# First unit of a seven-product matmul kernel: position 3 ahead of position 2, W11 loaded in four pieces, sums of W1 on VectorE, idle transposes at the start, logits' transposes later

## The chip, the cores and the metric

The kernel runs on one core of one Trainium2 chip. A core has TensorE (PE in the profile; its weight loads are PEld), VectorE (DVE), ScalarE (ACT), GpSimd (POOL), SyncE (SP, which here only issues DMAs) and 16 DMA engines. The metric is the device time of the one core in microseconds (us). Lower is better. All numbers come from measured executions or from one profiled execution of the program.

## The reference

The input u has shape (4, 1024, 1024); everything is float32. What matters of the reference:

```
xn = layernorm(u)                                   # over the last axis
g  = sigmoid(xn @ gate_w.T + gate_b);  u_g = xn * g
y  = c * G * cumsum(b * u_g / G) + (d + mean(u_g) @ lr_u @ lr_v / 4) * u_g
h  = silu(xn @ w1.T);  h = silu(h @ w3.T);  h = h @ w2.T
routes = top-2 of softmax(xn @ wr.T) over 8 experts; gates = the two, normalised
out_ffn[:] = 0;  out_ffn[expert] += gate * h        # summed over all 4096 tokens, so only rows 0..7 differ from 0
return u + y * silu(out_ffn)                        # rows 8.. are just u
```

Only eight rows of the result differ from the input, but the routed sum runs over all 4096 tokens, so the products with w1 and w3 are computed in full. The product with w2 is made once, after the sum. The gate is needed for the first 1024 tokens alone.

## The kernel before, in words

**Units.** Work is cut in nine units n of 1024x1024x1024: units 0 to 3 multiply the four batches by w1, unit 4 is the gate, units 5 to 8 multiply h by w3. The plan works with 2x2 blocks of 512 and takes seven block products instead of eight. The seven are the positions i = 0..6; each needs a sum or difference of x blocks (steps "T") and one of weight blocks (steps "S"). Positions are grouped in chains that share an accumulator bank: `CHAINS = ((0, 1), (2,), (3, 4), (5, 6))`. A position has four tiles j, each 128 output rows by 512 columns, contracted over four slices k of 128.

**Precision.** Each operand is split into a rounded part and a rest. "WH" and "HI" are ScalarE's rounded copies (weights, x), "WO" and "LO" are VectorE's subtractions for the rest. A tile is three matmuls per k (lines 944 to 946), so 12 matmuls of 512 columns. PSUM has five banks for tiles (`main`), two for logits (`lgp`) and one `spare`. VectorE or ScalarE empties a finished tile (step "PO") into `s1`, `u3` or the output tile `o`; the step "ST" then stores tiles that are final.

**Unit 0** is special: x comes as rows, is normalised on the chip and transposed. There are eight row blocks t of 128 tokens. "ROW" loads one (512 KB), "NA" computes its mean and variance on VectorE (bn_stats) and GpSimd (the power -0.5), "NS" does the same with ScalarE sums and GpSimd, "NB" normalises on VectorE, "TR" transposes on TensorE (two groups of four), "TE" copies the result out of PSUM on ScalarE (two copies per group for t < 4, one for t >= 4), "TL" makes the rest on VectorE. Position 0 of unit 0 is done in two halves of 256 columns, steps "MP" (half, j). Position 2 needs f = a - b + d of the x blocks: steps "TQ" (two VectorE operations per t), then "HQ" (rounded copy) and "LZ" (rest). "XS" stores x blocks for unit 4.

**Order.** `plan()` writes one list of steps by hand. Every engine walks that list and does its own part of each step, strictly in the order of the list, with semaphore waits. So a late step holds up everything behind it on its engine. The first part (lines 236 to 245) is written out; from then on the tiles follow in order and `at(n, i, j, step)` puts extra steps behind the tile (n, i, j).

**Other steps around the change.** "WL" loads a 512x512 block of weights (1 MB), in the order 11, 12, 22, 21 for w1. "SP" (lines 769 to 778) makes two sums of w1 blocks on GpSimd. "LQ" computes logits with TensorE, "LE" copies them to SBUF on ScalarE, "RA" transposes them back on TensorE, "RT" reduces them on VectorE. "STAT" are ScalarE's sums over rows of units 1 to 3, "MVC", "MV" and "BC" turn them into mean and rstd, "LN" (VectorE, two operations over 128x2048) normalises a block. `places_of` hands out nine buffers for x blocks.

Of the kernel before, what the change touches and what calls it, by code (L numbers as in the profile page):

```python
# [12 lines left out]
E = 8  # L13
# [30 lines left out]

CHAINS = ((0, 1), (2,), (3, 4), (5, 6))
CHAIN_OF = (0, 0, 1, 2, 2, 3, 3)
# [20 lines left out]
def lo_place(n, i):  # L67
    return "l2" if n == 0 and i == 2 else LO_PLACE[i]
# [6 lines left out]
def plan():  # L75
# [7 lines left out]
    for n in range(NN):  # L83
        ln = 0 < n < GATE
        if n == 0:
            at(0, 1, 0, "TR", 6)
            at(0, 1, 0, "TE", 6, 0)
            at(0, 1, 0, "TE", 6, 1)
            at(0, 1, 0, "TQ", 2)
# [3 lines left out]
            at(0, 1, 1, "TQ", 3)  # L93
            for t in range(4):
                at(0, 1, 2, "HQ", t)
                at(0, 1, 2, "LZ", t)
# [28 lines left out]
            at(0, 3, 2, "RT", 0)
            at(0, 5, 0, "RT", 1)
        else:
# [97 lines left out]
    for k in range(3):  # L225
# [10 lines left out]
    steps = [("ROW", 0), ("ROW", 1), ("ROW", 2), ("WL", 0, 2, "11"), ("ROW", 3), ("ROW", 4), ("ROW", 5), ("WL", 0, 6, "12"),  # L236
# [9 lines left out]
    gate_tiles = [(i, j) for i in OUT_OF for j in range(4)]  # L246
    tiles = [(n, i, j) for n in range(NN) for i in range(7) for j in range(4)]

    def behind(k):

        if k < 0:
            return
        n, i, j = tiles[k]
        if n or i:
            steps.append(("PO", n, i, j))

# [13 lines left out]
    for k, (n, i, j) in enumerate(tiles):  # L270
# [3 lines left out]
        out_of(k - 2)  # L274
        if j == 1:
# [3 lines left out]
        steps.extend(extra.pop((n, i, j), []))  # L279
# [11 lines left out]
def places_of(steps):  # L291
# [11 lines left out]
    for s in steps:  # L303
# [8 lines left out]
        elif s[0] == "HI":  # L312
# [3 lines left out]
        elif s == ("TQ", 0):  # L316
            take(0, "f")
        elif s == ("HQ", 0):
            take(0, "h2", "l2")
        if s == ("T", 0, 4):  # L320
            free.append((place[(0, "f")], s))
        elif s[0] in ("ST", "GX") and s[2:] == (4, 3):
            free.append((place[(s[1], "o")], ("o", s[1])))
        elif s == ("MP", 1, 3) or s[0] == "MM" and s[3] == 3:
            n, i = s[1:3] if s[0] == "MM" else (0, 0)
            for name in (f"h{i}", lo_place(n, i)):
                free.append((place[(n, name)], 7 * n + i))
# [9 lines left out]
def program(nc, x, xT, wB, w2T, small, out):  # L337
# [43 lines left out]
    with ExitStack() as ctx:  # L381
# [115 lines left out]
        s_pa = sem("s_pa")  # L497
        s_pv = sem("s_pv")
# [69 lines left out]
        def vacated(wait, n, name):  # L568
# [21 lines left out]
        def x_in(wait, n, i):  # L590
# [3 lines left out]
            elif n == 0 and i == 2:  # L594
# [4 lines left out]
        def s_in(wait, w, k):  # L599

            if w == 0 and k in (1, 3):
                wait(s_sp, nth("SP", 0, k))
            else:
                wait(s_s, nth("S", w, k))
# [36 lines left out]
        def bank_free(wait, n, i, j):  # L641
# [3 lines left out]
            if was[1] < 2:  # L645
                wait(s_pa, pa(*was))
            else:
# [16 lines left out]
        def _(eng):  # L664
            wait = Waiter(eng)
            ncopy = 0
            for s in steps:
                kind = s[0]
                if kind == "ROW":
# [5 lines left out]
                    eng.dma_start(row_buf(r), x[r * P:(r + 1) * P, :]).then_inc(s_row[r if r < 8 else 4 + r % 2], 16)  # L675
                elif kind == "CST":
# [64 lines left out]
        def _(eng):  # L741
# [20 lines left out]
            for s in steps:  # L762
# [44 lines left out]
        def _(eng):  # L807
# [14 lines left out]
            for s in steps:  # L822
                kind = s[0]
                if kind == "TE":
# [7 lines left out]
                    eng.activation(xf(0, b)[:, :, ts], bk, ACT.Copy).then_inc(s_ter, 1)  # L832
                elif kind == "HQ":
                    t = s[1]
                    vacated(wait, 0, "h2")
                    wait(s_tq, nth("TQ", t))
                    ts = slice(t * P, (t + 1) * P)
                    eng.activation(xr(0, "h2")[:, :, ts], xf(0, "f")[:, :, ts], ACT.Copy).then_inc(s_hq, 1)
# [8 lines left out]
                elif kind == "WH":  # L847
                    w, p = s[1:]
                    src = w_from(w, p)
                    if p in (0, 1, 4):  # L850
                        wait(s_wl[{0: 2, 1: 6}.get(p, p) if w == 0 else p], wloads[(w, {0: 2, 1: 6}.get(p, p) if w == 0 else p)])
                    else:
                        s_in(wait, w, {5: 1, 2: 2, 3: 3, 6: 4}[p])
                    if w == 0 and p >= 4:
                        wait(s_tr, 2 * (8, 4, 2)[p - 4])
                    eng.activation(w_r(p, 0), src, ACT.Copy).then_inc(s_wh, 1)
                elif kind == "PO":
                    n, i, j = s[1:]
# [80 lines left out]
        def _(eng):  # L939
            wait = Waiter(eng)  # L940
            wait(s_id, 2)
# [6 lines left out]
            for s in steps:  # L948
                kind = s[0]
                if kind == "TR":  # L950
# [4 lines left out]
                    for h in range(2):  # L955
                        for q in range(4):
                            k = 4 * h + q
                            mm = eng.transpose(tr_banks(t)[h][:, q * P:(q + 1) * P], row_buf(t)[:, k * P:(k + 1) * P],
                                               ident[:, :])
                        mm.then_inc(s_tr, 1)  # L960
                elif kind == "MP":
                    half, j = s[1:]
                    wait(s_wo, nth("WO", 0, 0))
                    wait(s_tel, nth("TL", 2 * half + 1, 0))
                    ts = slice(2 * P * half, 2 * P * (half + 1))
                    xh, xl = xr(0, "h0"), xr(0, "l0")
                    wh, wl = w_r(0, 0), w_r(0, 1)
                    js = slice(j * P, (j + 1) * P)
                    for k in range(4):
                        mm = three(main[bank[(0, 0, j)]][:, ts], wh[:, k, js], wl[:, k, js], xh[:, k, ts], xl[:, k, ts],  # L970
                                   half == 0 and k == 0, False)
                    if half:
                        mm.then_inc(s_mm, 1)
# [422 lines left out]
```

## Time and profile before

| | us |
|---|---|
| median of 3 runs | 793.51 (792.91 to 794.73) |
| the profiled execution, its own time | 793.97 |
| span of its trace, first to last instruction | 792.2 |
| TensorE busy | 756.0 |
| VectorE busy | 514.2 |
| ScalarE busy | 353.0 |
| GpSimd busy | 54.0 |
| DMA, mean over the span | 148 GB/s |

Times in the rows are us from the start of the span. The busy time of TensorE is no measure of its speed: it is also busy at half clock. What counts is when a position starts, and how long TensorE takes from there to the next.

### The profile page before, as it was taken

The page shows a single profiled execution, that of the slowest core. Times are in us where ns is not written, and L with a number is a line of the kernel's source. Part 1 is how long each engine was busy: PE and PEld are TensorE (multiplying, and loading weights), DVE is VectorE, ACT ScalarE, POOL GpSimd, SP SyncE. Part 2 cuts the span into 40 slices and gives each one's busy share as a digit, 9 for nine tenths or more (in the row PEclk, how much of TensorE's full clock was granted, in tenths as well). Part 3 has the DMA queues.
Part 4 walks back from the last instruction along what each step waited for, and adds up shares of the span by engine and source line. Part 5 has one row for each costly group of instructions (what it writes and reads, how often), then busy time and mean ns, then how long its engine had stood idle before and what let it go on. Part 6 is the DMA issues. An engine that isn't in the chain of part 4 may idle for free.

```text
span 792.2 us, 8750 instructions
## 1 busy us (share of the span) xinstructions
PE 756.0 (95%) x3510; PEld 595.8 (75%) x3510; DVE 514.2 (65%) x557; ACT 353.0 (45%) x459; POOL 54.0 (7%) x57
## 2 busy tenths in 40 slices
PE   2889999799999999999998999999999999999996
PEld 2767886588778877888887877877787778777873
DVE  5689877666676758728799999475624553455322
ACT  6678846724675434423582346223323241334121
POOL 2530022102030200000000000000000000000000
PEclk9999999899999999999999999999999999999999
DMA  9634556245624353555775652304230414110500
GB/s 359 232 146 149 200 201 211 84 152 184 218 85 156 117 195 113 187 208 165 289 284 180 231 208 107 134 0 186 85 139 16 186 39 154 47 54 0 214 1 2
DMA packets 26968, 117.20 MB, mean 148 GB/s; under 512 B 3392, under 2 KB 3632, under 8 KB 19760
## 3 DMA queue, kind: packets, MB, share of 16 engines
q1 hardware_dynamic: 17712, 99.87, 34.5%
q10 hardware_dynamic: 9216, 16.78, 5.7%
q8 instruction: 27, 0.44, 0.2%
q14 instruction: 13, 0.11, 0.0%
HBM read 95.60 MB, written 37.77 MB: 168 GB/s over the span
## 4 chain that ended last, share of the span: by engine, by line
PE 77%; DVE 13%; issue 3%; ACT 3%; DMA 2%; POOL 1%; SPq 0%; ACTq 0%; DVEq 0%; POOLq 0%
PE main L944 24%; PE main L945 23%; PE main L946 23%; PE lgp L1005 1%; DVE x5f L1091 1%; DMA wl6f<-wB 1%; PE spare L1032 1%; PE lgp L1032 1%; DVE x4f L1091 1%; DMA wh5f<-x 1%; DVE x8f L1091 1%; DVE s L1091 1%; DVE x0r L1091 1%; DVE x3r L1091 1%; DVE rows L1134 1%
## 5 line engine op out<-in xcount | busy, mean ns | idle before, releaser
L1091 DVE TENSOR_TENSOR s<-s,main 128x512 f32<-128x512 f32 x72 | 48.9, 683 | 67.0 <-PE main L946 66.8
L1091 DVE TENSOR_TENSOR u<-u,main 128x512 f32<-128x512 f32 x36 | 24.5, 686 | 50.7 <-PE main L946 50.7
L879 ACT ACTIVATE s<-s 128x512 f32<-128x512 f32 x32 | 20.1, 630 | 58.2 <-DVE s L1091 58.2
L879 ACT ACTIVATE u<-u 128x512 f32<-128x512 f32 x32 | 20.1, 632 | 58.2 <-DVE u L1091 58.2
L1091 DVE TENSOR_TENSOR u<-s,main 128x512 f32<-128x512 f32 x36 | 24.4, 684 | 30.6 <-PE main L946 30.5
L879 ACT ACTIVATE rows<-rows 128x512 f32<-128x512 f32 x16 | 10.1, 632 | 67.9 <-DVE rows L1091 67.8
L864 ACT ACTIVATE s<-main 128x512 f32<-128x512 f32 x36 | 20.7, 593 | 41.9 <-PE main L946 21.7
L1091 DVE TENSOR_TENSOR rows<-s,main 128x512 f32<-128x512 f32 x16 | 11.0, 688 | 31.2 <-PE main L946 31.2
L820 ACT ACTIVATE rows<-rows,nm 128x1024 f32<-128x1024 f32 x24 | 27.7, 1153 | 0.8
L818 ACT ACTIVATE rows<-rows 128x1024 f32<-128x1024 f32 x26 | 27.3, 1050 | 0.1
L879 ACT ACTIVATE u<-main 128x512 f32<-128x512 f32 x32 | 18.7, 590 | 18.3 <-PE main L946 18.3
L945 PE MATMUL main<-x3r,wh0r 128*128 128x256 f32 (+1 forms) x64 | 22.5, 352 | 0.0
L944 PE MATMUL main<-x2r,wh0r 128*128 128x256 f32 (+1 forms) x48 | 17.0, 353 | 4.4 <-DVE x3r L1091 4.4
L804 POOL MEMSET tail<- 128x1024 f32 x1 | 1.0, 954 | 269.1 <-PE main L946 269.1
L792 POOL TENSOR_SCALAR mvu<-acs 128x4 f32<-128x4 f32 x6 | 5.9, 981 | 193.6 <-ACT rows L820 193.6
L946 PE MATMUL main<-x2r,wl0r 128*128 128x256 f32 (+1 forms) x48 | 16.2, 338 | 0.0
L944 PEld LDWEIGHTS main<-x2r,wh0r 128*128 128x128 f32 x48 | 10.2, 212 | 5.4 <-DVE wl0r L1091 4.8
L945 PEld LDWEIGHTS main<-x3r,wh0r 128*128 128x128 f32 x64 | 13.2, 207 | 1.2
L944 PE MATMUL main<-x2r,wh2r 128*128 128x512 f32 x32 | 12.9, 402 | 0.6 <-DVE x3r L1091 0.6
L945 PE MATMUL main<-x4r,wh4r 128*128 128x512 f32 x32 | 13.2, 412 | 0.0
L944 PE MATMUL main<-x4r,wh3r 128*128 128x512 f32 x32 | 12.6, 392 | 0.0
L946 PE MATMUL main<-x2r,wl2r 128*128 128x512 f32 x32 | 12.5, 390 | 0.0
(691 smaller groups left out, 2443.7 us busy)
## 6 DMA issues: line engine op xcount, KB each, us to landing
out<-x SPq DMA_DIRECT2D x31, 512.0 KB, 7.8
rows<-x SPq DMA_DIRECT2D x26, 512.0 KB, 4.2
H_d<-u ACTq DMA_DIRECT2D x32, 256.0 KB, 3.7
H_d<-s ACTq DMA_DIRECT2D x16, 256.0 KB, 2.9
rows<-xh_d SPq DMA_DIRECT2D x16, 256.0 KB, 4.9
w2f<-w2T SPq DMA_DIRECT2D x2, 2048.0 KB, 11.2
wl2f<-wB SPq DMA_DIRECT2D x3, 1024.0 KB, 8.3
wl6f<-wB SPq DMA_DIRECT2D x3, 1024.0 KB, 8.3
```

Source lines behind the costliest of these rows:

```text
L792: eng.tensor_scalar(mvu[:, h, 0, :], acs[:, h, 0, :], 1.0 / D, None, ALU.mult)
L818: link(eng.activation(row, row, ACT.Copy, accum_out=total))
L820: return eng.activation(where, row, ACT.Square, bias=nm[:, 0:1], accum_out=square)
L864: eng.activation(s1[:, j, :], bk, ACT.Copy).then_inc(s_pa, 1)
L879: ins = eng.activation(dst, src, ACT.Silu)
L944: eng.matmul(o, sh, mh, start=first, stop=False, skip_group_check=True)
L945: eng.matmul(o, sh, ml, start=False, stop=False, skip_group_check=True)
L946: return eng.matmul(o, sl_, mh, start=False, stop=last, skip_group_check=True)
L1005: mm = eng.matmul(lgp[h][Q * q:Q * (q + 1), :], wr32[:, NQ * kh + q, :], xf(n, b)[:, q, :], start=(kh == 0), stop=(kh == 1))
L1032: mm = eng.matmul(acc[o][Q * j:Q * (j + 1), :], Pz[:, 8 * u + 4 * h + j, :], c_buf(n, i, j), start=(u == 0 and h == 0), stop=(u == NU - 1 ...
L1091: return eng.tensor_tensor(o, a, b, op)
L1134: eng.tensor_scalar(row_buf(t), row_buf(t), mv0[:, t, 0:1], mv0[:, t, 1:2], ALU.subtract, ALU.mult).then_inc(s_nb, 1)
```

## The change

- The chains of unit 0 become (0, 1), (3,), (2,), (4,), (5, 6): position 3 (x part d - b) comes before position 2. Position 3's tiles are copied to `u3` by ScalarE, position 2's are added to `s1` by VectorE, position 4 adds `u3`, and a new step "PU" adds `s1` to `u3`. The per-t path TD, HQ, LZ now serves position 3 with one subtraction per t; f = a + (d - b) is one whole operation later (T, 0, 2).
- W11 comes as four 256 KB DMAs (W0) ahead of rows 2 and 3, with its own split steps WH0 and WO0, and MP goes by (half, k) with all four j inside, so that a piece k is enough to start.
- Block 21 of w1 goes to another buffer; the sums 1 and 3 of w1 move from GpSimd ("SP", removed) to VectorE ("S").
- 34 transposes of the identity into `spare` open TensorE's list ("WARM").
- NA and NS are dealt out anew, and the extra steps of unit 0 are moved.
- Around unit 1: HI and LO of its first blocks, LN a, LQ a and c, RA of its second logits and the STAT rows stand at other tiles.

```diff
-CHAINS = ((0, 1), (2,), (3, 4), (5, 6))   # still used for n > 0
+CHAINS0 = ((0, 1), (3,), (2,), (4,), (5, 6))
...
         if n == 0:
             at(0, 1, 0, "TR", 6)
+            at(0, 1, 0, "LZ", 0)
             at(0, 1, 0, "TE", 6, 0)
             at(0, 1, 0, "TE", 6, 1)
-            at(0, 1, 0, "TQ", 2)
+            at(0, 1, 0, "LZ", 1)
+            at(0, 1, 0, "NB", 7)
+            at(0, 1, 0, "TD", 2)
+            at(0, 1, 0, "HQ", 2)
+            at(0, 1, 0, "WO", 0, 3)
...
+            at(0, 1, 3, "T", 0, 2)
+            at(0, 1, 3, "S", 0, 1)
...
+            at(0, 2, 0, "S", 0, 2)
+            at(0, 2, 0, "HI", 0, 2)
+            at(0, 2, 0, "WH", 0, 2)
+            at(0, 2, 0, "LO", 0, 2)
+            at(0, 2, 1, "WO", 0, 2)
             for b in "acbd":
-                at(0, 2, 0, "LQ", 0, b)
+                at(0, 2, 1, "LQ", 0, b)
+            at(0, 2, 2, "T", 0, 4)
             at(0, 2, 2, "HI", 0, 4)
+            at(0, 2, 3, "T", 0, 1)
+            at(0, 2, 3, "LE", 0)
+            at(0, 3, 0, "S", 0, 4)
...
-            at(n, *((-1, 0) if first else (-2, 2)), "LO", n, 0)
-            at(n, *((-1, 3) if first else (-1, 0)), "HI", n, 1)
+            at(n, *((-1, 1) if first else (-2, 2)), "LO", n, 0)
+            at(n, *((-1, 2) if first else (-1, 0)), "HI", n, 1)
...
-                at(n, *((-2, 1) if first else (-4, 3)), "LN", n, "a")
+                at(n, *((-2, 3) if first else (-4, 3)), "LN", n, "a")
...
-                at(n, *((0, 0) if first else (-1, 1)), "LQ", n, "a")
-                at(n, *((0, 0) if first else (-1, 1)), "LQ", n, "c")
+                at(n, *((0, 1) if first else (-1, 1)), "LQ", n, "a")
+                at(n, *((0, 1) if first else (-1, 1)), "LQ", n, "c")
...
-                at(n, 2, 0, "RA", c + 1)
+                at(n, *((3, 0) if first else (2, 0)), "RA", c + 1)
...
-                when = [(0, i, j) for i, j in ((2, 0), (2, 0), (2, 2), (3, 0), (3, 2), (4, 0), (4, 2), (5, 0))]
+                when = [(0, i, j) for i, j in ((2, 1), (2, 3), (3, 0), (3, 1), (3, 3), (4, 0), (4, 2), (4, 3))]
...
-    steps = [("ROW", 0), ("ROW", 1), ("ROW", 2), ("WL", 0, 2, "11"), ("ROW", 3), ("ROW", 4), ("ROW", 5), ("WL", 0, 6, "12"),
-             ("ROW", 6), ("ROW", 7), ("WL", 0, 4, "22"), ("WL", 0, 3, "21"), ("CST", 0),
-             ("NA", 0), ("NS", 1), ("NA", 2), ("NB", 0), ("TR", 0), ("TE", 0, 0), ("TE", 0, 1), ("NB", 1), ("TR", 1), ("WH", 0, 0),
...
+    steps = [("WARM", 0), ("ROW", 0), ("ROW", 1)] + [("W0", k) for k in range(4)] + [("ROW", 2), ("ROW", 3), ("WL", 0, 6, "12"),
+             ("ROW", 4), ("ROW", 5), ("ROW", 6), ("ROW", 7), ("WL", 0, 5, "21"), ("WL", 0, 4, "22"), ("CST", 0),
+             ("NA", 0), ("NA", 1), ("NB", 0), ("TR", 0), ("NB", 1), ("TR", 1),
+             ("WH0", 0), ("WH0", 1), ("WH0", 2), ("WH0", 3), ("TE", 0, 0), ("WO0", 0), ("TL", 0, 0), ("NA", 2), ("TE", 1, 0), ("TL", 1, 0),
+             ("TE", 0, 1), ("TE", 1, 1), ("WO0", 1), ("WO0", 2), ("NA", 3), ("NB", 2), ("WO0", 3),
+             ("MP", 0, 0), ("MP", 0, 1), ("TR", 2), ("MP", 0, 2), ("MP", 0, 3), ("NA", 5), ("NB", 3), ("TR", 3),
+             ("NS", 4), ("TE", 2, 0), ("TE", 2, 1), ("NA", 6), ("TL", 2, 0), ("TE", 3, 0), ("TL", 3, 0), ("TE", 3, 1),
+             ("MP", 1, 0), ("MP", 1, 1), ("NB", 4), ("TR", 4), ("MP", 1, 2), ("MP", 1, 3), ("WH", 0, 1),
+             ("XS", "a"), ("XS", "c"), ("TL", 0, 1), ("TL", 1, 1), ("TL", 2, 1), ("TL", 3, 1), ("NB", 5), ("TR", 5), ("WO", 0, 1),
+             ("TE", 4, 0), ("TE", 4, 1), ("NS", 7), ("PO", 0, 0, 0), ("PO", 0, 0, 1), ("PO", 0, 0, 2), ("PO", 0, 0, 3),
+             ("TE", 5, 0), ("TE", 5, 1), ("NB", 6), ("TD", 0), ("HQ", 0), ("S", 0, 3), ("WH", 0, 3), ("TD", 1), ("HQ", 1), ("ROW", 8), ("ROW", 9)]
...
+                elif kind == "W0":
+                    k = s[1]
+                    eng.dma_start(w_f(2, 1)[:, k, :], wB[0, 0, 0, :, k, :]).then_inc(s_w0[k], 16)
...
-                elif kind == "SP":
-                    k = s[2]
-                    for p in (3, 4) if k == 1 else (2,):
-                        wait(s_wl[p], wloads[(0, p)])
-                    if k == 1:
-                        ins = eng.tensor_tensor(w_f(5, 1), w_f(3, 1), w_f(4, 1), ALU.add)
-                    else:
-                        wait(s_sp, 1)
-                        ins = eng.tensor_tensor(w_f(3, 1), w_f(2, 1), w_f(3, 1), ALU.subtract)
-                    ins.then_inc(s_sp, 1)
...
+                if kind == "WARM":
+                    wait(s_id, 1)
+                    for q in range(34):
+                        eng.transpose(spare[:, q % 4 * P:(q % 4 + 1) * P], ident[:, :], ident[:, :])
+                    wait(s_id, 2)
...
+                elif kind == "PU":
+                    j = s[1]
+                    wait(s_p3, j + 1)
+                    wait(s_pv, pv(0, 2, j))
+                    tt(u3[:, j, :], u3[:, j, :], s1[:, j, :], ALU.add).then_inc(s_pv, 1)
```

In unit 0 the second argument of `at` is now the rank in the chain order, so `at(0, 2, ...)` stands at position 3 and `at(0, 3, ...)` at position 2.

## Rows read from the trace of the kernel before

**Rows 1.** Page, part 1: busy us, share of the span, instructions.
```profile
PE 756.0 (95%) x3510; PEld 595.8 (75%) x3510; DVE 514.2 (65%) x557; ACT 353.0 (45%) x459; POOL 54.0 (7%) x57
```

**Rows 2.** Waits of TensorE, whole run: us in total, times, longest us.
```profile
PE main L958 <- DVE wh6f L1134: 10.3, 1, 10.3
PE main L944 <- DVE x3r L1091: 5.0, 2, 4.4
PE lgp L1012 <- ACT lg L912: 4.6, 1, 4.6
PE lgp L958 <- DVE rows L1134: 3.9, 1, 3.9
PE main L944 <- DVE wl1r L1091: 2.3, 1, 2.3
```

**Rows 3.** Windows: length, busy (x) per engine, clock, DMA share, GB/s.
```profile
31.54:43.27 11.73, 5.52 (x32) 5.34 (x33) 11.73 (x5) 7.90 (x17) 10.89 (x4) 0.85 0.36 124
...
57.44:117.77 60.33, 60.33 (x285) 46.83 (x286) 49.69 (x38) 45.29 (x68) 5.78 (x6) 1.00 0.52 187
117.77:144.87 27.10, 26.70 (x133) 18.84 (x132) 21.77 (x12) 16.48 (x29) 6.64 (x3) 1.00 0.50 175
144.87:164.49 19.62, 15.05 (x54) 11.44 (x55) 10.65 (x8) 12.06 (x17) 0.00 (x0) 0.83 0.34 120
...
164.49:175.37 10.88, 10.88 (x49) 9.01 (x48) 6.98 (x7) 4.40 (x6) 0.00 (x0) 1.00 0.42 146
```

**Rows 4.** Timeline of VectorE: start, us, instruction, idle before.
```profile
30.38 5.01 DVE L1134 TENSOR_SCALAR rows<-rows,mv 128x1024 f32<-128x1024 f32 x1 [2.11 <-POOL mv L785]
...
43.09 2.28 DVE L1091 TENSOR_TENSOR wh6f<-wl5f,wl2f 128x2048 f32<-128x2048 f32 x1
...
66.10 0.68 DVE L1091 TENSOR_TENSOR s<-s,main 128x512 f32<-128x512 f32 x1
```

**Rows 5.** Timeline of GpSimd.
```profile
30.31 4.53 POOL L774 TENSOR_TENSOR wl5f<-wl3f,wl4f 128x2048 f32<-128x2048 f32 x1
```

**Rows 6.** Timeline of all engines, first 10 us.
```profile
3.95 0.69 DVE L1128 BATCH_NORM_STATS2 bst<-wh6f 128x6 f32<-128x512 f32 x1 [3.95 <-DMA wh6f<-x]
...
5.25 1.06 ACT L818 ACTIVATE wh6f<-wh6f 128x1024 f32<-128x1024 f32 x1 [3.23 <-DMA wh6f<-x]
...
5.89 0.58 POOL L768 TENSOR_TENSOR mv<-mv,mhalf 128x1 f32<-128x1 f32 x1
...
7.96 0.69 DVE L1128 BATCH_NORM_STATS2 bst<-wh5f 128x6 f32<-128x512 f32 x1 [2.48 <-DMA wh5f<-x]
...
9.41 1.48 DVE L1134 TENSOR_SCALAR wh6f<-wh6f,mv 128x1024 f32<-128x1024 f32 x2
```

**Rows 7.** DMA issues on SyncE: start, us to issue.
```profile
2.13 0.44 SPq L683 DMA_DIRECT2D wl2f<-wB  x1
...
4.32 1.19 SPq L683 DMA_DIRECT2D wl6f<-wB  x1
```

**Rows 8.** DMA issues, first 12 us: KB each, median us to landing.
```profile
wl2f<-wB SPq DMA_DIRECT2D x1, 1024.0 KB, 8.3
...
wl6f<-wB SPq DMA_DIRECT2D x1, 1024.0 KB, 12.4
```

**Rows 9.** Timeline of ScalarE.
```profile
24.53 0.60 ACT L830 ACTIVATE x2r<-lgp 128x512 fp32r<-128x512 f32 x1 [0.31 <-PE lgp L958]
...
26.45 1.08 ACT L818 ACTIVATE rows<-rows 128x1024 f32<-128x1024 f32 x1
...
29.04 1.90 ACT L856 ACTIVATE wh1r<-wl6f 128x2048 fp32r<-128x2048 f32 x1
...
48.51 1.28 ACT L879 ACT_TABLE_LOAD   x1
```

**Rows 10.** Chain of waits, start and us: two matmuls of 256 columns.
```profile
19.35 0.21 PE main L944
...
22.87 0.12 PE main L946
```

More of the change, by code:

```diff
@@ L67, in lo_place, with chains, order, rank @@
 def lo_place(n, i):
-    return "l2" if n == 0 and i == 2 else LO_PLACE[i]
+    return f"l{i}" if n == 0 and i in (2, 3) else LO_PLACE[i]
+def chains(n):
+    return CHAINS if n else CHAINS0
+def order(n):
+    return [i for c in chains(n) for i in c]
+def rank(n, i):
+    return 7 * n + order(n).index(i)
 def layer_of(n):
@@ L255, in behind @@
             steps.append(("PO", n, i, j))
+        if n == 0 and i == 2 and j == 3:
+            for t in range(4):
+                steps.append(("PU", t))
     def out_of(k):
@@ L274, in plan @@
         out_of(k - 2)
+        p = rank(n, i) % 7
         if j == 1:
@@ L315, in places_of @@
             take(s[1], "f")
-        elif s == ("TQ", 0):
+        elif s == ("TD", 0):
             take(0, "f")
         elif s == ("HQ", 0):
+            take(0, "h3", "l3")
+        elif s == ("HI", 0, 2):
             take(0, "h2", "l2")
-        if s == ("T", 0, 4):
-            free.append((place[(0, "f")], s))
+        if s in (("T", 0, 4), ("T", 0, 1)):
+            free.append((place[(0, "f" if s[2] == 4 else "b")], s))
         elif s[0] in ("ST", "GX") and s[2:] == (4, 3):
@@ L488, in program @@
         s_t = sem("s_t")
+        s_w0 = [sem(f"s_w0{k}") for k in range(4)]
+        s_wh0 = sem("s_wh0")
+        s_wo0 = sem("s_wo0")
         s_wh = sem("s_wh")
@@ L573, in vacated @@
                 wait(s_t, nth(*was))
+                wait(s_hi, nth("HI", 0, 2))
+                wait(s_lo, nth("LO", 0, 2))
+            elif was == ("T", 0, 1):
+                wait(s_t, nth(*was))
+                wait(s_lq, nth("LQ", 0, "b"))
+                wait(s_xs[2], 16)
             elif isinstance(was, tuple):
@@ L599, in s_in, with w_in, mm @@
         def s_in(wait, w, k):
-            if w == 0 and k in (1, 3):
-                wait(s_sp, nth("SP", 0, k))
-            else:
-                wait(s_s, nth("S", w, k))
+            wait(s_s, nth("S", w, k))
+        def w_in(wait, w, i):
+            if w == 0 and i == 0:
+                wait(s_wo0, 4)
+            else:
+                wait(s_wo, nth("WO", w, i))
+        def mm(n, i, j):
+            return 4 * rank(n, i) + j + 1
         def pv(n, i, j):
@@ L646, in bank_free @@
                 wait(s_pa, pa(*was))
+            elif was[:2] == (0, 3):
+                wait(s_p3, was[2] + 1)
             else:
@@ L967, in _ @@
                     wh, wl = w_r(0, 0), w_r(0, 1)
[L968 to L973, printed above, removed]
+                    for j in range(4):
+                        js = slice(j * P, (j + 1) * P)
+                        ins = three(main[bank[(0, 0, j)]][:, ts], wh[:, k, js], wl[:, k, js], xh[:, k, ts], xl[:, k, ts],
+                                    half == 0 and k == 0, False)
+                        if half and k == 3:
+                            ins.then_inc(s_mm, 1)
                 elif kind == "MM":
@@ L978, in _ @@
                     bank_free(wait, n, i, j)
-                    if n == 0 and i == 2:
+                    if n == 0 and i == 3:
                         wait(s_ter, 16)
-                    wait(s_wo, nth("WO", w, i))
+                    w_in(wait, w, i)
                     x_in(wait, n, i)
@@ L985, in _ @@
                     js = slice(j * P, (j + 1) * P)
-                    begins = i in (0, 2, 3, 5)
+                    begins, ends = (i in [c[e] for c in chains(n)] for e in (0, -1))
                     for k in range(4):
-                        first, last = begins and k == 0, not begins and k == 3 or i == 2 and k == 3
+                        first, last = begins and k == 0, ends and k == 3
                         if n < L2:
-                            mm = three(o, wh[:, k, js], wl[:, k, js], xh[:, k, :], xl[:, k, :], first, last)
+                            ins = three(o, wh[:, k, js], wl[:, k, js], xh[:, k, :], xl[:, k, :], first, last)
                         else:
-                            mm = three(o, xh[:, k, js], xl[:, k, js], wh[:, k, :], wl[:, k, :], first, last)
-                    mm.then_inc(s_mm, 1)
+                            ins = three(o, xh[:, k, js], xl[:, k, js], wh[:, k, :], wl[:, k, :], first, last)
+                    ins.then_inc(s_mm, 1)
                 elif kind == "LQ":
@@ L1169, in _ @@
                         raw_in(wait, n, X_FROM[i])
+                    elif (n, i) == (0, 2):
+                        vacated(wait, 0, "l2")
+                        wait(s_t, nth("T", 0, 2))
                     elif i != 6:
@@ L1189, in _ @@
                             wait(s_xs[0], 16)
+                            wait(s_t, nth("T", 0, 2))
                         if n < GATE:
@@ L1192, in _ @@
                         ins = tt(a, b, a, ALU.subtract)
+                    elif (n, k) == (0, 2):
+                        raw_in(wait, 0, "a")
+                        wait(s_hq, 4)
+                        wait(s_lz, 4)
+                        ins = tt(xf(0, "f"), xf(0, "f"), a, ALU.add)
                     elif k == 2:
@@ L1283, in _ @@
                         dst = c_buf(n, 4, j)
+                        if n == 0:
+                            wait(s_pv, pv(0, 3, j))
+                            old = u3[:, j, :]
                     elif i == 5:
```

175 lines of the change are left out of this document (91 added, 84 removed), and 7 rows, old and new, of the table steps.

## The prediction

> **What bounds the kernel now.** I read the busy shares first, then TensorE's waits, then the windows between the starts of positions, and last the queues of VectorE, ScalarE and GpSimd where a wait ends. TensorE is busy 95% of the span [rows 1], so only two things can move the time: TensorE waiting, and TensorE at half clock. Of the waits, five lie before unit 1 has passed its third position [rows 2]: 10.3 us for the first normalised rows, 4.4 of the 5.0 us for the first rest of x and of W11, 3.9 for the normalised row block 3, 2.3 for the rest of W12, and 4.6 in unit 1 for the copy of the logits. In steady state a position takes 10.88 us, the window 164.49:175.37 [rows 3]; position 2 of unit 1 took 19.62, at a mean clock of 0.83 [rows 3]. The 3.9 us wait has its cause on GpSimd: VectorE's normalisation, which takes 0.74 us elsewhere (1.48 for two) [rows 6], took 5.01 while GpSimd ran its sum of 128x2048, 4.53 us [rows 4, 5]. In 31.54:43.27 GpSimd and VectorE are busy side by side for 10.9 us and TensorE only for 5.5 [rows 3]. All the rest behind 164.49 is untouched by the diff.
>
> **The walk through the new start.** I go through the new list engine by engine. Units of cost: a ScalarE copy of 128x512 0.48 (four between 24.53 and 26.45), NS 2.59 (26.45 to 29.04), a weight copy 1.9 [rows 9]; a VectorE operation over 128x2048 2.2, over 128x512 0.61 (2.28 and 0.68 less 0.07 overlap with the next) [rows 4]; NA 1.5 (two of 0.69 and the aggregate, estimated 0.2), NB 0.74, GpSimd's part 0.9 [rows 6]. A matmul of 256 columns is 0.12 at full and 0.21 at half clock [rows 10], so MP of one k (12 matmuls) is 1.43 or 2.56, and a TR of eight transposes about 0.9 or 1.75 (estimated, a transpose being as long as a 256-column matmul).
>
> *Loads.* R1 is there at 5.25, R2 at 7.96 [rows 6]; W11, with 2.62 MB issued up to it, at 2.13 + 8.3 = 10.4, W12, with 5.24 MB, at 4.32 + 12.4 = 16.7 [rows 7, 8]. By the same bytes the last piece of W11 now lands at about 9.2 (2.1 MB), R2 10.4, R3 11.7, R4 15.3, R5 16.7, R6 17.8, R7 18.9. Bounds for the pieces: 7.6 (in strict order) to 10.4. The four issues take 0.44 each [rows 7], faster than the data flow.
>
> *Rows 0 and 1.* NA 0 from 3.95, NA 1 from 5.5 to 7.0, NB 0 to 7.8: today NB 0 stands behind NA 2, which waits for R2, and starts at 9.41 [rows 6]. TR 0 at 7.8 instead of 10.3, TR 1 9.3 to 10.2 (GpSimd's part beside NB 0 taken at up to 1.5). ScalarE rounds the pieces by 9.75, then TE 00 to 10.8, TE 10 to 11.8. VectorE: TL 00, NA 2 (R2), TL 10 to 13.6. So MP starts at **13.7**; before, the waits of 10.3 and 4.4 us stood ahead of it [rows 2].
>
> *Clock.* The 34 idle transposes start at about 1.6 and last 3.7 to 7.2 us, so they end by 8.8 at the latest; they cost at most 1 us on TR 0, hidden by the pieces. But TensorE then idles from 10.2 to 13.7, about 3.5 us. In this trace the clock fell to 1.2 GHz with the waits of 3.9 and 4.6 us: the mean clocks of the windows that hold them are 0.85 and 0.83, against 1.00 in the windows without such a wait [rows 2, 3]. I take the half clock for the first 3.6 us: +1.35 us on the walk below. The Trainium skill ("TensorE: Matmul & The Clock Gate", What's actually happening) says that the chip's look at activity runs free of the kernel, so that the same kernel warms at another matmul from run to run; by that the 1.35 could be 0 or double, and this trace can't decide it, being one execution.
>
> *Position 0.* At full clock: MP 00, 01 to 16.6; TR 2 (NB 2 at 17.0) to 18.0; MP 02, 03 to 20.9; TR 3 to 21.8; NS 4 holds ScalarE 15.3 to 17.9, TE 2 to 20.0, TE 30 at 22.4, TL 30 at 23.1; MP 10 at 23.25, then TensorE has work: MP 11 26.1, TR 4 27.0, MP 12, 13 29.85, TR 5 30.75. ScalarE's NS 7 and PO(0,0,0) end at 30.7, so position 1 starts at **30.8** (43.27 before: the end of that window). W12's copy and rest are ready at 29.2.
>
> *Position 1* takes 10.9 and two TR (1.8). TR 7 waits for NB 7 behind LZ 1, behind HQ 1 (ScalarE, 36.0): 0.3 us of stall. TE 7 comes behind PO(0,1,0) with the table load of 1.28 [rows 9], and HQ 3, LZ 3 end at 43.0. Position 3 starts at **43.8**, with the half clock at **45.2**; today the third position starts at 57.44. The sum that this took from GpSimd, S 3, is at 30.6 to 32.8 on VectorE beside MP and PO: hidden; slack of its user WO(0,3) 4 us. **Gain of the front: 57.44 - 45.2 = 12.2** (bounds: 6, if the pieces land with today's W11, 1.2 us later, and ScalarE's queue slips by 5, two NS; and 13.6 with the clock held).
>
> *The five positions to unit 1* have the same content as in 57.44:117.77, 60.33 us without a wait [rows 3]. VectorE gets S 1, S 2, LO 2, WO 2, T 2 and four PU there (5 x 2.2 + 4 x 0.61 = 13.4 us) and loses WO 3, T 3, LO 3 (6.6). Walking VectorE's and ScalarE's lists I find the last operand of position 2 ready 4 us ahead, of position 4 3 us, of position 5 5 us, of position 6 6 us. The tightest is LO(1,0): LN a starts 13.2 us before unit 1, then LN c, PO, LO(1,0) end 0.7 us before it. Cost 0 (up to 1.5 if it slips). Cover gone, each us late is a us of stall.
>
> *Unit 1.* RA of its second logits goes from the first tile of position 2 to that of position 3, some 11 us later, and the copy that it waited for was 4.6 late: the wait goes. With it goes the half clock behind it. Position 2 should take 10.88 + 0.7 (RA, MV) = 11.6 instead of 19.62: 8.0; the 0.4 idle in 117.77:144.87 (27.10 against 26.70 busy) goes too, since VectorE reaches LO 2 about 23 us after the start of the unit, position 2 being due at 25.8. **Gain 8.4** (bounds 0 and 8.4). Moving the STAT rows costs nothing: ScalarE is busy 45 of 60 us there, and their last is due 8 us before the mean is used.
>
> *Sum:* 12.2 + 8.4 = 20.6. Own time of the profiled execution 793.97 - 20.6 = 773.4; the median of the runs is 0.46 below that execution, so **773.0**.
>
> **Rivals.**
> - *The boundary wait only moves.* LO(1,0) or HI(1,1) slips past its 0.7 us, since LN a now comes two tiles later and VectorE has more to do; TensorE then waits some 4 us and comes back at half clock as it did behind RA. For: the thin slack. Against: each of VectorE's durations is measured and it idled here before. Gain 12.2 + 0.4: 793.5 - 12.6 = **781**.
> - *ScalarE sets the pace of the front.* NS 4, TE 2 and 3, NS 7 and PO(0,0,0) stand in one queue with no slack at 30.7. A row that lands 2 us later and 2 to 4 us of such slips leave a front gain of about 7: 793.5 - 15.4 = **778**.
> - *Slower than before: TensorE stays at 1.2 GHz until position 3.* The front now has many short waits (before MP, TR 2, TR 3, MP 10, TR 7) where the old one had a few long ones. At half clock 96 matmuls cost 0.09 more, 8.6, 48 of 512 columns 0.2 more, 9.6, eight TR 0.85 more, 6.8: 25.0, of which 1.35 is counted: 773.0 + 23.6 = **797**. It turns slower from about 20 of these 25 us on. For: the mean clock of 0.85 today. Against: from MP 10 on there is work without a gap, and every window without a long wait has a mean clock of 1.00 [rows 3].
> - *The front's gain is given back at unit 1*: LN a there waits for the sums of its rows (STAT 8 to 11, GpSimd, MV, BC) and their loads, which come no earlier. Against: by the walk they have 4 us or more to spare. Unit 1's gain alone stays: 793.5 - 8.4 = **785**.
>
> **How the numbers follow.** Forecast 0.55 (its own range 770 to 776), ScalarE 0.20, boundary 0.17, loads of the sums 0.05, half clock 0.03. The range 768 to 782 holds the first three but for their tails; its low end adds the held clock (1.35) and the doubts of the walk on the good side. Runs of this kernel can tell 0.2% (1.6 us) from no change: faster 0.95, same 0.02, slower 0.03.
>
> **What would show it.** MP's first matmul near 13.7; its spacing there 0.21 or 0.12; position 1 at 31 to 32, position 3 at 44 to 46, unit 1 at 104 to 107; no GpSimd row over 128x2048; no NB above 1 us; no wait of L1012 in unit 1 and position 2 there in about 11.6 us. Wrong would be a new wait of more than 1 us between position 3 of unit 0 and position 3 of unit 1, or a first MP behind 16.

## The result, and the profile after

The changed kernel takes 775.0 us, the median of 4 runs (774.69 to 776.75), beside 793.21 us (792.54 to 794.73) for the kernel before on the same chip: ratio 0.9772, 95% interval 0.9752 to 0.9793. It is 18.2 us faster, where 20.5 were forecast (773.0), and the time lies in the range of 768 to 782. The profiled execution took 776.75 us with a span of 774.8 (792.2 before).

The page of the kernel after, part 1, answers to [rows 1]: TensorE's busy time is the same 756 us, its share is 98% instead of 95.

```profile
PE 756.1 (98%) x3544; PEld 596.9 (77%) x3544; DVE 510.9 (66%) x567; ACT 347.4 (45%) x451; POOL 40.3 (5%) x52
```

TensorE's waits, whole run of the kernel after (us in total, times, longest), answer to [rows 2]:

```profile
PE main L995 <- DVE x3r L1147: 6.6, 2, 5.1
PE main L995 <- DVE u L1147: 2.0, 1, 2.0
PE spare L1004 <- POOL ident L798: 1.6, 1, 1.6
...
PE main L1014 <- DVE wh6f L1190: 0.8, 1, 0.8
PE lgp L1014 <- DVE wh6f L1190: 0.4, 1, 0.4
```

The waits of 10.3, 3.9, 2.3 and 4.6 us are gone. One of 5.1 us stands ahead of the first MP, and one of 1.5 (6.6 less 5.1) ahead of MP (1, 0); the walk of the prediction has this second one too, from 21.8 to 23.25. The windows of the kernel after, cut where positions start (columns as in [rows 3]):

```profile
15.43:20.72 5.29, 5.29 (x25) 5.29 (x26) 5.22 (x11) 2.75 (x6) 2.42 (x4) 0.50 1.04 422
20.72:35.21 14.49, 13.00 (x106) 12.53 (x105) 11.32 (x17) 10.04 (x18) 3.51 (x8) 0.97 0.73 289
35.21:48.34 13.13, 13.08 (x64) 10.58 (x65) 9.39 (x11) 11.24 (x18) 2.58 (x3) 1.00 0.25 92
48.34:108.66 60.32, 60.32 (x286) 46.77 (x286) 53.77 (x40) 47.98 (x74) 3.73 (x6) 1.00 0.61 209
108.66:135.12 26.46, 26.46 (x133) 19.09 (x132) 23.74 (x12) 16.52 (x28) 6.51 (x3) 1.00 0.53 185
135.12:146.54 11.42, 11.42 (x51) 9.03 (x50) 7.05 (x7) 11.29 (x16) 0.00 (x0) 1.00 0.37 127
146.54:157.89 11.35, 11.35 (x54) 9.40 (x52) 8.42 (x7) 4.76 (x8) 0.00 (x0) 1.00 0.60 221
```

Read down the lengths: this is where the time came from. The starts before are those of the trace before.

| stretch | before | forecast | after | gained |
|---|---|---|---|---|
| to the first MP | 18.36 | 13.7 | 15.43 | 2.93 |
| first MP to position 1 | 24.91 | 18.45 | 19.78 | 5.13 |
| position 1 to the third position | 14.17 | 13.05 | 13.13 | 1.04 |
| five positions to unit 1 | 60.33 | 60.33 | 60.32 | 0.01 |
| unit 1 to its position 4 | 57.60 | 49.2 | 49.23 | 8.37 |
| the rest of the span | 616.83 | same | 616.91 | -0.08 |

The sum is 17.40, the difference of the spans (792.2 - 774.8).

How far can one trace be trusted with such starts? Two of the kernels below (a_ra_back, a_sums_on_gpsimd) leave TensorE's work up to position 1 as it is in the changed kernel, and start position 1 at 34.36 and 33.80 instead of 35.21. Two others (b_unit1_all, b_ra_only) do the same with the kernel before and start it at 43.90 and 42.59 instead of 43.27. So a difference of up to 1.4 us in the start of position 1 between two single traces shows nothing by itself.

### The profile page after: what moved, and what is told of

Its sections match the earlier page's. It is cut to its first block, busy times and chain, and to the rows that moved or that the text cites. A ratio compares the mean times of both kernels' runs of the same rounds, so it can differ in the third digit from the quotient of the medians.

```text
span 774.8 us, 8825 instructions
## 1 busy us (share of the span) xinstructions
PE 756.1 (98%) x3544; PEld 596.9 (77%) x3544; DVE 510.9 (66%) x567; ACT 347.4 (45%) x451; POOL 40.3 (5%) x52
## 4 chain that ended last, share of the span: by engine, by line
PE 85%; DVE 8%; issue 3%; DMA 2%; ACT 2%; SPq 0%; DVEq 0%
PE main L995 27%; PE main L997 26%; PE main L996 26%; PE lgp L1061 2%; DMA wl6f<-wB 1%; PE spare L1088 1%; DMA wl2f<-wB 1%; PE lgp L1088 1%; DVE x3r L1147 1%; DVE s L1147 1%; DVE x3f L1147 1%; DVE x0r L1147 1%; DVE x1r L1147 1%; DVE u L1379 1%; PE main L1122 0%
## 5 line engine op out<-in xcount | busy, mean ns | idle before, releaser
L1147 DVE TENSOR_TENSOR u<-s,main 128x512 f32<-128x512 f32 x32 | 21.7, 682 | 29.6 <-PE main L997 29.6
L912 ACT ACTIVATE s<-main 128x512 f32<-128x512 f32 x36 | 20.5, 594 | 44.5 <-PE main L997 19.0
L931 ACT ACTIVATE u<-main 128x512 f32<-128x512 f32 x32 | 18.6, 590 | 17.6 <-PE main L997 17.4
L995 PE MATMUL main<-x6r,wh3r 128*128 128x512 f32 x32 | 12.5, 392 | 0.0
L996 PE MATMUL main<-x6r,wh0r 128*128 128x512 f32 x32 | 12.5, 390 | 0.0
L996 PE MATMUL main<-x5r,wh1r 128*128 128x512 f32 x32 | 12.5, 390 | 0.0
L997 PE MATMUL main<-x6r,wl3r 128*128 128x512 f32 x32 | 12.5, 389 | 0.0
L996 PE MATMUL main<-x5r,wh2r 128*128 128x512 f32 x32 | 12.5, 389 | 0.0
```

The source lines that it names most:

```text
L931: ins = eng.activation(dst, src, ACT.Silu)
L995: eng.matmul(o, sh, mh, start=first, stop=False, skip_group_check=True)
L996: eng.matmul(o, sh, ml, start=False, stop=False, skip_group_check=True)
L997: return eng.matmul(o, sl_, mh, start=False, stop=last, skip_group_check=True)
L1147: return eng.tensor_tensor(o, a, b, op)
```

## The experiments

Each run is beside the kernel before on its chip; its time is the median of 4 or 5 runs. Code cuts are marked with "...".

**Unit 1's moves alone, on the kernel before.**

```diff
-                at(n, 2, 0, "RA", c + 1)
+                at(n, *((3, 0) if first else (2, 0)), "RA", c + 1)
...  # and the changed places of HI, LO, LN a, LQ a and c, STAT rows; nothing else of the change
```

> The kernel before with only the moves around unit 1 (HI, LO, LN a, LQ a and c, RA, STAT rows). My theory: this group is worth 8.4 us by itself, whatever the front does, so the ratio to before is 0.9895 (about 784.9 us), unit 1 up to its position 3 takes about 38 us instead of 46.7, and no wait of the logits' transpose is left. Rival: without the earlier start of the front the moves only shift VectorE's work and the wait comes back at LO of unit 1; then 788 to 793.

Measured: 785.83 (before 793.55), ratio 0.9903 (0.9886 to 0.9919). Unit 1 runs from 118.64 to its position 4 at 167.87, 49.23 us, the very figure of the changed kernel. The stage is 8.4 us shorter by the trace (57.60 before) and the median 7.7 lower; the 785.8 is 0.9 above what I expected, and position 1 starts 0.6 later in this trace, which is scatter. The group doesn't need the new front.

**RA alone, on the kernel before.** Only the changed line above.

> The kernel before with RA of unit 1's second logits alone moved from the first tile of position 2 to that of position 3. Theory: the wait of 4.6 us and the half clock behind it go with this one step, so 785.5 (8.0 less). Rival: the ScalarE copy it waited for is a sign of a late VectorE; then LO 2 or LO 3 of unit 1 makes TensorE wait instead, and only some 3 us are won (790).

Measured: 786.73, ratio 0.9915 (0.9899 to 0.9932). Position 2 of unit 1 takes 11.54 us instead of 19.62, by this kernel's window:

```profile
130.07:144.17 14.10, 13.70 (x69) 9.48 (x68) 13.86 (x8) 6.92 (x12) 6.28 (x3) 1.00 0.27 95
144.17:155.71 11.54, 11.54 (x50) 9.11 (x51) 6.84 (x5) 9.38 (x12) 0.00 (x0) 1.00 0.32 113
```

So one step moved by 11 us brings 7.6 of the 8.4 us (unit 1 to position 4: 49.99), and 6.8 by the medians, 1.2 less than I expected. The 0.4 us of idle in front of position 2 stays (14.10 against 13.70): that is what the other moves of the group remove, with another 0.35 in the stretches around.

**RA back, in the changed kernel.** The same line the other way.

> The changed kernel with RA of unit 1's second logits back at the first tile of position 2. In the changed kernel that tile ends at 137.9 and the copy that RA needs ends at about 140.1. Theory: a wait of 2.3 us comes back, without or with half clock behind it: 777.3 to 780. Rival: the earlier HI, LO and LQ steps alone removed the wait: 775.

Measured: 780.24 (777.79 to 781.59), ratio 0.9818 (0.9791 to 0.9845), a little above the 777.3 to 780 of the expectation. The wait returned, and with it, in this trace, the half clock:

```profile
PE lgp L1068 <- ACT lg L964: 2.4, 1, 2.4
```

Its window of position 2:

```profile
134.28:151.71 17.43, 14.98 (x55) 11.37 (x54) 8.59 (x7) 11.91 (x17) 0.00 (x0) 0.80 0.40 137
```

17.43 instead of 11.42: 2.4 of wait, 0.5 for the transposes themselves, which stand in position 3 otherwise (10.88 here, 11.35 there), and 3.1 of half clock. The four runs differ: two near 781.6 with a mean granted clock of 0.988 over the run, two at 777.8 and 778.9 with 0.992. The trace has the first kind: from unit 1 to its position 4 it takes 54.78 instead of 49.23, so a wait of 2.4 us cost 5.5. That in the other two the wait stood without the half clock is read from their mean clocks and times only; no trace shows it.

**The sums on VectorE, in the kernel before.**

```diff
-                        ins = eng.tensor_tensor(w_f(5, 1), w_f(3, 1), w_f(4, 1), ALU.add)       # GpSimd
+                        ins = tt(w_f(5, 1), w_f(3, 1), w_f(4, 1), ALU.add)                      # VectorE, same place; the other sum too
```

> The kernel before with its two GpSimd sums of W1 done by VectorE at the same two places. Theory: both engines were slowed by each other for 10.9 us; VectorE now needs 4.4 us more of its own and loses about 9 of stretched time, NB 3 takes 0.8 instead of 5.0, position 1 starts about 5 us earlier and no half clock follows: 787 to 789. Rival: VectorE was the bound of the front anyway, so its 4.4 us come in the place of the 3.9 us wait: 792 to 794.

Measured: 788.87, ratio 0.9944 (0.9927 to 0.996). Its VectorE, at the place of [rows 4]:

```profile
30.01 0.81 DVE L1124 TENSOR_SCALAR rows<-rows,mv 128x1024 f32<-128x1024 f32 x1 [2.12 <-POOL mv L775]
30.74 2.28 DVE L1081 TENSOR_TENSOR wl5f<-wl3f,wl4f 128x2048 f32<-128x2048 f32 x1
33.13 2.29 DVE L1081 TENSOR_TENSOR wl3f<-wl2f,wl3f 128x2048 f32<-128x2048 f32 x1
```

The normalisation takes 0.81 instead of 5.01 and each sum 2.3 where GpSimd took 4.5 to 4.8. Position 1 starts at 38.93 instead of 43.27 (42.59 and 43.90 in the two other traces with the front of before), and the third position at 53.32 instead of 57.44: some 4 us of the front come from this edit alone, 4.7 by the medians. Not as expected, half clock did follow: a wait of 4.0 us for the rest of W12 now stands ahead of position 1, where 2.3 stood, and position 1 has a mean clock of 0.88.

**The sums on GpSimd, in the changed kernel.**

```diff
-                elif kind == "S":                                       # VectorE
+                elif kind == "S" and s[1:] not in ((0, 1), (0, 3)):
...
+                elif kind == "S" and s[1:] == (0, 3):                   # GpSimd; (0, 1) alike
...
+                    eng.tensor_tensor(w_f(3, 1), w_f(2, 1), w_f(5, 1), ALU.subtract).then_inc(s_sp, 1)
```

> The changed kernel with sums 1 and 3 of W1 put back on GpSimd, at the places that the changed kernel gives them. Theory: sum 3 (near 35 us) now stretches VectorE's rest of W12, NB 6, NB 7 and the TD and LZ steps by some 4 us and position 1 or 3 starts 2 to 4 us later: 777 to 779. Rival: at those places VectorE has slack, so within 1 us of the changed kernel (775 to 776).

Measured: 782.0, ratio 0.986 (0.9843 to 0.9876), 7 us slower than the changed kernel, where I expected 2 to 4. GpSimd, then VectorE of this kernel, then TensorE's wait:

```profile
34.46 4.61 POOL L838 TENSOR_TENSOR wl3f<-wl2f,wl5f 128x2048 f32<-128x2048 f32 x1
39.15 4.85 POOL L842 TENSOR_TENSOR wl5f<-wl5f,wl4f 128x2048 f32<-128x2048 f32 x1
```

```profile
36.22 3.40 DVE L1163 TENSOR_TENSOR x8f<-x7f,x6f 128x512 f32<-128x512 f32 x1 [2.88 <-ACT x7f L889]
39.54 5.61 DVE L1163 TENSOR_TENSOR x3r<-x8f,x2r 128x512 fp32r<-128x512 f32 x2
```

```profile
PE lgp L1030 <- DVE wh4f L1206: 5.5, 1, 5.5
```

Three VectorE operations of 0.7 us each last 9 us. Position 1 takes 20.38 us instead of 13.13, with a mean clock of 0.83. I had counted one sum in reach; both ran there, one behind the other: GpSimd had no other step between them. That this is why the edit costs more in the new order than it gave in the old is argued, not tried.

**Without the idle transposes.**

```diff
-                    for q in range(34):
+                    for q in range(0):
```

> The changed kernel without the 34 transposes of the identity. In the changed kernel the first MP started at 15.43, at half clock, after an idle stretch of about 5 us. Theory: the transposes only make TR 0 and TR 1 faster (about 0.5 instead of 0.9 us per four), and MP waits for the copies behind the pieces of W11; so 0 to 0.7 us slower (775 to 775.7), and the first two MP take as long as now (5.3 us). Rival: they pay for the whole front, 2 us or more slower.

Measured: 775.12 (774.62 to 776.17), ratio 0.9767 (0.9749 to 0.9786): no difference. TR 0 and TR 1 end later (3.65 us of transposes from 8.14 instead of 2.05 from 7.71), and the first MP starts at 15.27 all the same. MP 00 and 01 take 4.85 us here and 5.29 in the changed kernel, beside 4.81 and 4.80 in a_ra_back and a_sums_on_gpsimd, which have the transposes. The transposes of the change buy nothing, as expected.

**Kept busy up to MP.**

```diff
+                    if t == 1:
+                        for q in range(46):
+                            eng.transpose(main[q % 4][:, 0:P], ident[:, :], ident[:, :])
```

> The changed kernel with 46 more transposes of the identity behind TR 1, into banks that MP then begins anew. Theory: the half clock of the first two MP (24 matmuls at 0.22 instead of 0.12) comes from the idle stretch ahead of them; kept busy, MP 00 and 01 take 2.9 instead of 5.3 us. What follows waits for rows 4 (ScalarE's NS 4, on its DMA), so of the 2.4 us between 0.5 and 2.4 come through: 772.6 to 774.5. Rival: the clock falls anyway or MP is late behind the added transposes: 775 to 776.

Measured: 775.27 (774.85 to 775.61), ratio 0.9764 (0.9747 to 0.9781): no difference, where I expected 0.5 to 2.4 us. The rival's time came, but not for its reason, since the clock held and MP was not late. The window of the first two MP in this kernel:

```profile
15.36:18.40 3.04, 3.04 (x28) 2.97 (x27) 3.01 (x7) 1.40 (x4) 1.30 (x2) 1.00 1.02 404
```

3.0 instead of 5.3 us, so the half clock there was the idle stretch's doing. From the first MP to position 1 it is 17.05 us instead of 19.78, 2.7 less, since TR 2 behind MP 01 ran at half clock as well. Position 1 starts at 32.41 instead of 35.21 and unit 2 at 190.40 instead of 193.19, yet the span is only 1.2 us shorter and the median not at all. Where the other 1.6 went: position 4 of the gate unit took 13.38 instead of 14.89 (1.5 better), and against that stood a new wait of 1.05 us on the gate's VectorE work, 0.7 in unit 5 and 1.25 in the tail. The tails, 9.07 after and 10.32 here, with the same work:

```profile
765.73:774.80 9.07, 3.60 (x32) 1.53 (x32) 1.54 (x3) 1.18 (x3) 0.00 (x0) 0.88 0.02 4
```

```profile
763.28:773.60 10.32, 4.87 (x32) 1.64 (x32) 1.54 (x3) 1.18 (x3) 0.00 (x0) 0.76 0.01 3
```

**W11 as one DMA.**

```diff
-                    eng.dma_start(w_f(2, 1)[:, k, :], wB[0, 0, 0, :, k, :]).then_inc(s_w0[k], 16)
+                    if k == 0:
+                        eng.dma_start(w_f(2, 1), wB[0, 0, 0]).then_inc(s_w0[0], 16)
...  # and the steps that use the pieces wait for this one load
```

> The changed kernel with W11 as one DMA of 1 MB at the same place in the queue (WH0 and WO0 still in four). The traces show the first piece at 7.9 and the others at about 9.75, and the rows behind some 2 us later than bytes alone would have them. Theory of the prediction: the split brings the first copy forward and costs no rate: with one DMA everything on ScalarE starts at about 9.8 to 10, TE 00 0.5 to 1 us later, 776 to 777. Rival: the short pieces cost DMA rate (mean 279 against 316 GB/s in the first 12 us); one DMA brings rows 2 to 7 forward by 1 to 2 us, and the time is the same or better (773 to 775).

Measured: 774.96 (774.84 to 775.9), ratio 0.9765 (0.9748 to 0.9783). ScalarE of the changed kernel, then of this one:

```profile
7.92 0.63 ACT L877 ACTIVATE wh0r<-wl2f 128x512 fp32r<-128x512 f32 x1 [5.90 <-DMA wl2f<-wB]
9.78 1.91 ACT L877 ACTIVATE wh0r<-wl2f 128x512 fp32r<-128x512 f32 x3 [1.22 <-DMA wl2f<-wB]
11.59 0.58 ACT L871 ACTIVATE x2r<-main 128x512 fp32r<-128x512 f32 x1
...
17.37 1.06 ACT L859 ACTIVATE rows<-rows 128x1024 f32<-128x1024 f32 x1 [1.79 <-DMA rows<-x]
```

```profile
9.25 2.19 ACT L878 ACTIVATE wh0r<-wl2f 128x512 fp32r<-128x512 f32 x4 [7.23 <-DMA wl2f<-wB]
11.35 0.57 ACT L872 ACTIVATE x2r<-main 128x512 fp32r<-128x512 f32 x1
...
15.60 1.06 ACT L860 ACTIVATE rows<-rows 128x1024 f32<-128x1024 f32 x1 [0.27 <-DMA rows<-x]
```

The whole block is there at 9.25, before the last of the four pieces could be used; row 4 comes 1.8 us earlier. The time came out as the rival said (773 to 775), not as the theory (776 to 777). Position 1 starts at 33.49 instead of 35.21, but row 4 has no part in that: 0.25 us is the first MP (15.18), 1.0 is MP 00 and 01 in 4.29 instead of 5.29 us, 0.45 is TR 2, at half clock there and not here, and from MP (1, 0) to position 1 both take 7.8. In the changed kernel ScalarE, done with row 4, still waits for TR 2:

```profile
21.81 0.60 ACT L871 ACTIVATE x2r<-main 128x512 fp32r<-128x512 f32 x1 [1.78 <-PE main L1014]
```

In the median the one DMA makes no difference. That the short pieces cost DMA rate is seen in this pair of traces only.

**The first copies ahead of the last pieces.** In the changed kernel ScalarE ends the four pieces at 11.59 and only then empties TR 0, which was done at 8.8. The edit moves three steps: ScalarE's copies TE 00 and TE 10 ahead of three pieces, and VectorE's TL 10 ahead of NA 2. They were not tried one by one.

```diff
-             ("WH0", 0), ("WH0", 1), ("WH0", 2), ("WH0", 3), ("TE", 0, 0), ("WO0", 0), ("TL", 0, 0), ("NA", 2), ("TE", 1, 0), ("TL", 1, 0),
+             ("WH0", 0), ("TE", 0, 0), ("TE", 1, 0), ("WH0", 1), ("WH0", 2), ("WH0", 3), ("WO0", 0), ("TL", 0, 0), ("TL", 1, 0), ("NA", 2),
```

> The changed kernel with ScalarE copying TR 0's and TR 1's first group (TE 00, TE 10) before the last three pieces of W11, and VectorE making TL 10 before NA 2. Theory: MP 00 waits for exactly this queue; it starts near 12 instead of 15.4, and the clock does not fall in the shorter gap. But NS 4 still waits for row 4 at about 17 in front of TE 2, so position 1 starts only 2 to 3 us earlier: 772 to 774. Rival: MP 01 to 03 wait for the pieces instead and nothing is won (775).

Measured: **772.89** (771.38 to 773.14), ratio 0.9736 (0.9721 to 0.9751): faster than both kernels. It is 2.1 us below the changed kernel's median; its slowest run (773.14) is below the fastest of the changed kernel (774.69), and the two intervals just miss each other (0.9751 and 0.9752). Windows from its first MP on:

```profile
11.94:16.64 4.70, 4.69 (x24) 4.45 (x24) 4.42 (x9) 2.72 (x6) 1.68 (x3) 0.64 1.02 422
16.64:31.35 14.71, 12.60 (x105) 12.12 (x105) 13.59 (x21) 12.41 (x23) 5.81 (x10) 1.00 0.99 397
```

MP starts at 11.94 and position 1 at 31.35. That is 3.9 us before the changed kernel and 2.5 to 3.0 before the two kernels named under the result that have the changed kernel's front, so the 2.1 us of the median are what to go by. That the clock would hold in the shorter gap was wrong: MP began at full clock (0.12 us a matmul), was at half from 12.3 to 15.7, and the window's mean is 0.64.

**NS 4 behind TE 2 and TE 3** as well:

```diff
-             ("NS", 4), ("TE", 2, 0), ("TE", 2, 1), ("NA", 6), ("TL", 2, 0), ("TE", 3, 0), ("TL", 3, 0), ("TE", 3, 1),
+             ("TE", 2, 0), ("TE", 2, 1), ("TL", 2, 0), ("TE", 3, 0), ("TL", 3, 0), ("TE", 3, 1), ("NA", 6), ("NS", 4),
```

> The same and NS 4 behind the copies TE 2 and TE 3. Theory: ScalarE no longer waits for row 4 in front of TE 2; MP 10 starts near 22 instead of 27.4 and position 1 some 5 us earlier than in the changed kernel: 770 to 772. Rival: NB 4 is late then (row 4's sums end near 22.5) and TR 4 waits, giving back 2 us: 772 to 774.

Measured: 775.79 (774.87 to 776.14), ratio 0.9777 (0.9763 to 0.9792): above the theory (770 to 772) and above the rival (772 to 774), 2.9 us slower than the swap alone. The rival's mechanism is there, larger than it was given. VectorE of this kernel, at NB 4:

```profile
26.98 0.81 DVE L1190 TENSOR_SCALAR rows<-rows,mv 128x1024 f32<-128x1024 f32 x1 [2.63 <-POOL mv L826]
```

NS 4 now starts at 23.0 behind the copies instead of at 17.2, where it filled ScalarE's wait for TR 2, and TR 4 waits for its row: 1.74 us of idle, 0.54 and 0.79 further on. Position 1 starts at 33.23 and unit 1 at 107.34, 1.9 and 2.55 us later than with the swap alone.

**NA 5 later too**, and **this with W11 as one DMA.** Edits: NA 5 behind NB 3, TR 3 and the copies and rests of TR 2 and TR 3; then the edit of the one DMA above as well.

> The same and NA 5 (which waits for row 5) behind NB 3 and the rests TL 2, TL 3. Theory: in the faster front VectorE would stand at NA 5 for its row; moved, TR 3 comes 1 to 2 us earlier: 769 to 771. Rival: no difference to the kernel with NA 5 in its place.

> The same with W11 as one DMA of 1 MB. Theory: now the first piece alone is needed early (7.9 against 9.3), so one DMA costs 1 us at MP 00, and gives back up to 1.5 at rows 4 and 5: within 1 us of the kernel with four pieces (769 to 772).

Measured: 775.49 (774.56 to 776.32), ratio 0.9774 (0.9759 to 0.979), and 774.94 (774.36 to 775.29), ratio 0.9769 (0.9756 to 0.9783). The 769 to 771 and 769 to 772 that I expected both failed, and the rival (no difference from NA 5) came. Both have the same wait of 1.75 us at NB 4, and position 1 at 33.27 and 33.85. So behind the late NS 4 the place of NA 5 makes no difference, and neither does the one DMA. Whether either would help beside the swap alone, with NS 4 in its old place, was not tried.

## Why the prediction was right, step by step

- **Unit 1: right in mechanism and size.** Forecast 8.4, measured 8.37, and shown by itself (b_unit1_all: 49.23 us with the old front). The step that does it is RA; the forecast that the half clock goes with the wait is shown from both sides, by taking the wait away and by bringing it back.
- **LO(1,0) and the boundary: right.** There is no wait between 48.34 and 157.89. LO(1,0) ends at 107.8 for a start of unit 1 at 108.66: 0.9 us to spare where the walk gave 0.7. That rival is out, and so is the one that the sums for LN a and their loads hold unit 1 up.
- **GpSimd's sums: right, and larger than the sum needed.** The prediction put the cost on the two engines slowing each other; both experiments show it, 4.7 us in the old front and 7 in the new one.
- **The front as a whole: 12.2 forecast, 9.1 measured.** The mechanism held, two sizes were off, and they make up all of the 3.1 that are missing:
  - *The first MP*, 13.7 against 15.43: the step "ScalarE rounds the pieces by 9.75" failed. Pieces 2 to 4 could be used only from 9.78 on, not 9.2, and their copies then took 1.8 us one behind the other, which my walk had let run alongside the loads; TE 00 began at 11.59 instead of 9.8. It is 1.7 us.
  - *The half clock*, 1.35 against 2.7: I had let the clock come back after 3.6 us, but the whole of MP 00 and 01 (5.29 us, mean clock 0.50) and the first half of TR 2 ran at 1.2 GHz. It is 1.4 us more than forecast. With the engine kept busy the stretch from the first MP to position 1 took 17.05, and the walk at full clock has 17.1, so nothing else in it was off.
  - *Row 4* came at 17.4 instead of 15.3 and cost nothing, since ScalarE waited for TR 2 behind it.
  - *The size of the half clock is in part luck*: in a_ra_back and a_sums_on_gpsimd the same stretch took 18.84 and 18.83, a cost of 1.8, and the prediction had said that 1.35 could be 0 or double.
- **What in the front brought the 9.1 us is shown in part.** The sums are worth some 4; the four pieces and the idle transposes nothing. Position 3 ahead of position 2, the new order of NA, NS and NB, and MP by k were not tried alone.
- **"The idle transposes cost nothing": right, but the other half was missing.** They are also worth nothing, since the engine idles 5.1 us behind them and what follows waits for ScalarE. The forecast of half clock in spite of them was right.
- **ScalarE sets the pace of the front:** this rival, with 0.20, came closest to what the front did. It was not a late row that slowed the queue, but the order in it, as the edit of a_te_first shows.
- **The half-clock rival** (797) did not come: from 20.72 to 157.89 every window has a mean clock of 0.97 or more.

That the medians moved 18.2 us and the spans 17.4 is within the scatter of the runs. The late positions scatter too: position 4 of the gate unit took 14.80 before and 14.89 after, 14.8 to 14.9 in the two traces in which RA's line alone is changed, and 13.3 to 13.4 in the ten others. What decides it was not tried.

## What to carry to other kernels

In a list that every engine walks in order, look for the step that waits for something not yet there while the step behind it could run: here one reordering of copies gave 2.1 us, four DMAs and 34 warming transposes nothing, and pushing such a step too far back cost 2.9. In this kernel a TensorE wait of 2 us or more costs the wait plus 0 to 3 us of half clock (3.1 behind the wait of 2.4, 3 behind that of 4.6, 2.7 behind the idle 5.1), and a GpSimd sum over whole tiles all but stops VectorE for as long as it lasts. A gain of 1 to 3 us in one stage can be lost to such waits elsewhere: read it in the stage's window, then ask the median.

## What the runs showed of the hardware

- GpSimd's 128x2048 sum of two operands takes 4.5 to 4.9 us beside a busy VectorE; in that time a VectorE 128x512 operation takes 2.8 to 3.4 instead of 0.69 and a 128x1024 normalisation 5.0 instead of 0.81. The small GpSimd operation in front of NB 7 took 2.28 us instead of 0.2 to 0.3 while VectorE ran a sum over 128x2048 (the rows below, of the kernel after).

```profile
34.67 2.28 DVE L1147 TENSOR_TENSOR wl3f<-wl2f,wl5f 128x2048 f32<-128x2048 f32 x1
34.76 2.28 POOL L824 TENSOR_SCALAR mv<-acs 128x1 f32<-128x1 f32 x1 [10.40 <-ACT wh3f L861]
```

- The same kernel gave two times 3 to 4 us apart with two mean clocks (RA back). That suggests that whether the clock falls behind a wait of 2.4 us is not fixed by the program; one of the two kinds has no trace.
- How long half clock lasts is not fixed by the program either: behind an idle stretch of 4.5 to 5.1 us the same 24 matmuls took 5.29, 4.81 and 4.80 us in three traces, and 2.98 where transposes of the identity filled the stretch (a_keep_busy; its window above holds the start of TR 2 too). The wait of 1.5 us ahead of MP (1, 0) was followed by full clock (MP (1, 0) at 0.12 us a matmul in the changed kernel).
